# The first tile's z transposed by four DMA transfers from ScalarE's queue, in place of 32 products by the identity

## Chip, core and metric

One core of a Trainium2 chip runs the whole kernel as one program. The metric is the device time in microseconds of one execution; the time before is the median of three.

## What is computed

The input x is 2048 tokens of 512 channels in fp32. Three layers follow each other, each with a residual: `x += 0.5*ffn(layernorm(x))`, then `x += s4(layernorm(x))` (a causal convolution along the channels with a kernel computed from the state-space parameters), then the same ffn again. The ffn is

```python
def _qlinear(x, q, scale, A, Bm):
    w = (q.astype(jnp.float32) - Q_ZERO) * (scale * Q_STEP)[:, None]
    return jnp.einsum('bsh,oh->bso', x, w) + LR_SCALE * (x @ A @ Bm)
g = _qlinear(x, gate_q, gate_scale, gate_A, gate_B)
u = _qlinear(x, up_q, up_scale, up_A, up_B)
h = jax.nn.silu(g) * u
return _qlinear(h, down_q, down_scale, down_A, down_B)
```

with H = 512, I = 1376 and rank 32. The weights q arrive as int32 values of 0 to 15.

## The kernel before

The program is written by hand, one instruction list for each engine, with semaphores between them; nothing is scheduled by a planner, so the order in each list is the order of execution. The 2048 tokens form four tiles of 512, each of four sub-tiles of 128 tokens; the two ffn layers make eight passes, `tile(0)` to `tile(7)`. Every fp32 operand of a product is split into a high and a low fp16 part, so each product runs twice. Tile 0 runs plain products (`plain_blocks`); from tile 1 on a seven-product scheme over 2x2 halves is used (`fast_blocks`), for which the weight sums are made during tile 0.

The normalized input, called z, has tokens on the partitions and has to be turned, so that channels lie on the partitions, before TensorE (PE) can multiply it by the weights. From tile 1 on the turning is done by DMA transposes that SyncE (SP) issues (`quarter_transpose`, L413 to L420). In tile 0 it is done on TensorE: for each sub-tile j VectorE (DVE) makes the fp32 z (`ln_scale`, L915), ScalarE (ACT) rounds it to the high part (`z_first_high`, L848), DVE subtracts to get the low part (`ln_low`, L923, which raises `f.z16`), TensorE multiplies the eight 128x128 blocks by an identity into one bank of PSUM (`x_transpose`, L1407), and one copy brings the 128x1024 result to `xT_plain` in SBUF: ACT's `x_out` (L697) for sub-tiles 0 and 2, DVE's `x_out` (L928) for 1 and 3. `f.xT0[j]` tells that a sub-tile is there.

Around it lies the start of the program. SP loads x, then the int32 weights in four chunks, the low-rank matrices and the constants, all from its own DMA queue (L355 to L386) while the first tile runs. ACT issues four small loads from its own queue at its very start (L646 to L649). TensorE runs `warm`, products of the identity by itself that nobody reads, until z is there (L1732 and L1734). Then it runs, in the order of L1735 to L1749: `p_product(0, i)` (eight products of one turned sub-tile by the low-rank A), `first_products(j)` (the sixteen products of one turned sub-tile with the first block of gate and of up weights) and `p_transpose`. After them `plain_blocks(0)` begins at L1541 with products over all 512 tokens (`product`, L1537).

What ties the engines there: ACT's list from L876 to L892 is `z_first_high`, `low_rank_a_high`, `x_out`, `cast_up` (int32 weights to fp16, L865, which waits for its chunk), `p_high` (three small copies of one low-rank result, L655, waits for `p_product`), `low_rank_b_high`, `p_out` (copies a turned p, L673) and again `cast_up`. `p_transpose(j)` on TensorE waits for `p_out(j-1)` (L1451), and the last of the four low-rank products waits for `p_split(0, 0)` on DVE, which waits for `p_high(0, 0)`. So TensorE cannot enter `plain_blocks(0)` before ACT has done `p_out(1)`, which stands last but one in ACT's list of the start.

## Time and profile before

| | |
|---|---|
| median of 3 runs | 569.65 us (569.47 to 571.22) |
| the profiled execution's own time | 569.99 us |
| its span, first to last instruction | 568.2 us |
| what lies around the span | 1.8 us |
| TensorE busy / VectorE / ScalarE / GpSimd | 556.5 / 427.2 / 312.9 / 256.4 us |

The busy time of TensorE is counted from modelled ends of pipelined products; the chain of waits shows in what order the work that ended last was released. Times are counted from the first instruction. Rows that end in SPq or ACTq are DMA issues: their duration is the time for which the issuing engine's sequencer was held, and the time to landing is counted from the start of the issue.

### The profile page before, as it was taken

What the parts mean: (1) busy time and instruction counts of PE and PEld (TensorE: products, weight loads), DVE (VectorE), ACT (ScalarE), POOL (GpSimd) and SP (SyncE); (2) the same over time, 40 slices, a digit from 0 to 9 for tenths busy, and PEclk for the clock granted to TensorE, in tenths of its full rate; (3) what the DMA queues carried; (4) which work ended last, traced back from release to release, by engine and by line L of the source; (5) the groups of instructions that cost most, each with busy time, mean ns of one, the idle gap of its engine ahead of it and who ended that gap; (6) DMA issues with size and microseconds to landing.
All of it is one profiled execution on the core that took longest, in us unless ns stands there. A gap on an engine that the chain in (4) does not pass through costs nothing.

```text
span 568.2 us, 12661 instructions
## 1 busy us (share of the span) xinstructions
PE 556.5 (98%) x4816; PEld 449.4 (79%) x4816; DVE 427.2 (75%) x824; ACT 312.9 (55%) x773; POOL 256.4 (45%) x272
## 2 busy tenths in 40 slices
PE   8999999989999999999999999999999999999997
PEld 8644678887688877888778887788877888788975
DVE  5789889996889957889578884598845987555544
ACT  5778425863168831688317883178731676246621
POOL 4379612664036850368503784037830477015510
PEclk9999999999999999999999999999999999999999
DMA  8985431009050190002900029000391104440002
GB/s 262 340 282 204 86 59 43 2 1 131 15 22 5 30 180 15 2 2 35 175 16 2 1 38 171 15 3 1 59 151 55 37 2 56 84 158 2 2 0 75
DMA packets 90804, 40.04 MB, mean 70 GB/s; under 512 B 79000, under 2 KB 84889, under 8 KB 90745
## 3 DMA queue, kind: packets, MB, share of 16 engines
q1 hardware_dynamic: 89849, 38.97, 31.3%
q8 instruction: 38, 0.62, 0.5%
q10 hardware_dynamic: 896, 0.27, 0.2%
q14 instruction: 21, 0.17, 0.1%
HBM read 15.90 MB, written 4.19 MB: 35 GB/s over the span
## 4 chain that ended last, share of the span: by engine, by line
PE 92%; DVE 5%; issue 1%; ACT 1%; DVEq 1%; POOL 0%; POOLq 0%; ACTq 0%
PE banks L1561 40%; PE banks L1480 28%; PE banks L1523 6%; PE banks L1537 5%; PE banks L1706 5%; PE banks L1432 2%; PE banks L1716 2%; PE banks L1500 1%; PE banks L1517 1%; PE banks L1726 1%; DVE X L1050 0%; DVE c_stats L1080 0%; DVE ring L1047 0%; DVEq L909 0%; PE banks L1415 0%
## 5 line engine op out<-in xcount | busy, mean ns | idle before, releaser
L1561 PE MATMUL banks<-xT,w 128*128 128x256 f16 (+1 forms) x2156 | 260.4, 273 | 1.5 <-DVE work L1006 1.4
L1561 PEld LDWEIGHTS banks<-xT,w 128*128 128x128 f16 (+1 forms) x2156 | 212.5, 100 | 26.3 <-DVE work L1006 2.7
L1480 PE MATMUL banks<-dw,hT 128*128 128x256 f16 (+3 forms) x1408 | 184.0, 286 | 0.0
L1480 PEld LDWEIGHTS banks<-dw,hT 128*128 128x128 f16 (+1 forms) x1408 | 135.4, 98 | 33.8 <-issue 0.4
L1006 DVE SCALAR_TENSOR_TENSOR work<-banks,work 128x512 f32<-128x512 f32 (+1 forms) x88 | 60.6, 688 | 43.4 <-PE banks L1523 27.4
L501 POOL TENSOR_TENSOR rstd<-veps,minus_half 128x1 f32<-128x1 f32 x32 | 19.6, 615 | 160.8 <-DVE veps L912 160.7
L571 POOL TENSOR_SCALAR hT<-work 128x512 f16<-128x512 f32 x70 | 44.2, 631 | 99.6 <-DVE work L1006 99.6
L574 POOL TENSOR_TENSOR hT<-work,hT 128x512 f16<-128x512 f32 x70 | 82.6, 1179 | 5.8
L1020 DVE SCALAR_TENSOR_TENSOR banks<-banks,scales,work 128x512 f32<-128x512 f32 (+1 forms) x77 | 57.7, 750 | 0.7 <-PE banks L1561 0.7
L1027 DVE SCALAR_TENSOR_TENSOR banks<-banks,scales,work 128x512 f32<-128x512 f32 (+1 forms) x77 | 57.7, 750 | 0.2 <-ACT work L807 0.2
L581 POOL TENSOR_TENSOR z<-zs,z 128x1024 f16<-128x1024 f32 (+1 forms) x28 | 55.5, 1992 | 4.5 <-ACT z L740 4.4
L793 ACT ACTIVATE work<-banks,scales 128x256 f32<-128x256 f32 (+1 forms) x77 | 36.6, 475 | 32.5 <-PE banks L1561 32.5
L807 ACT ACTIVATE work<-banks,scales 128x256 f32<-128x256 f32 (+1 forms) x77 | 36.5, 474 | 31.2 <-PE banks L1561 31.1
L686 ACT ACTIVATE pd_stack<-banks 128x32 f16<-128x32 f32 x96 | 11.8, 195 | 69.2 <-PE banks L1480 69.2
L723 ACT ACTIVATE work<-banks 128x512 f32<-128x512 f32 (+1 forms) x77 | 46.0, 597 | 5.7 <-PE banks L1523 5.7
L789 ACT ACTIVATE work<-banks,scales 128x256 f32<-128x256 f32 (+1 forms) x77 | 36.5, 474 | 7.4 <-PE banks L1561 7.4
L1537 PE MATMUL banks<-xT,w 128*128 128x512 f16 (+1 forms) x160 | 37.9, 379 | 0.6 <-ACT work L716 0.5
L694 ACT ACTIVATE PdT<-banks 128x128 f16<-128x128 f16 x32 | 8.9, 277 | 50.9 <-PE banks L1491 50.8
L796 ACT ACTIVATE work<-banks,scales 128x256 f32<-128x256 f32 (+1 forms) x77 | 36.5, 474 | 0.0
L996 DVE SCALAR_TENSOR_TENSOR pd_stack<-banks,pd_stack 128x32 f16<-128x32 f32 x32 | 6.0, 186 | 35.6 <-ACT pd_stack L686 35.4
L740 ACT ACTIVATE z<-zs 128x512 f16<-128x512 f32 (+1 forms) x56 | 29.8, 568 | 3.0 <-DVE zs L942 2.0
L1537 PEld LDWEIGHTS banks<-xT,w 128*128 128x128 f16 (+1 forms) x160 | 15.5, 100 | 19.8 <-ACT work L716 3.1
(191 smaller groups left out, 677.2 us busy)
## 6 DMA issues: line engine op xcount, KB each, us to landing
out_x<-X SPq DMA_DIRECT2D x15, 256.0 KB, 2.8
X<-in_x SPq DMA_DIRECT2D x1, 2048.0 KB, 9.9
ring<-in_gate_q_t SPq DMA_DIRECT2D x2, 768.0 KB, 9.5
hT<-in_up_q_t SPq DMA_DIRECT2D x2, 768.0 KB, 11.3
X<-in_b SPq DMA_DIRECT2D x2, 560.0 KB, 10.7
X<-in_x SPq DMA_DIRECT2D x1, 1024.0 KB, 14.3
ring<-in_down_q_t SPq DMA_DIRECT2D x1, 1024.0 KB, 12.5
X<-in_x SPq DMA_DIRECT2D x3, 256.0 KB, 5.0
```

Of the source, the lines that this page charges most:

```text
L571: pool.tensor_scalar(hT[0:r, m, 0, :], h32[0:r, b, :], 1.0, 0.0, ALU.mult, ALU.add)\
L574: pool.tensor_tensor(hT[0:r, m, 1, :], h32[0:r, b, :], hT[0:r, m, 0, :], ALU.subtract)\
L581: pool.tensor_tensor(z16[:, j, 1, ops, :], zs[:, ops, :], z16[:, j, 0, ops, :], ALU.subtract)\
L723: nc.scalar.activation(silu[0:r, b, :].rearrange("p (c t) -> p c t", c=2), gate_sums(m), ACT.Silu, scale=LR_OUT).then_inc(f.silu[b], 1)
L789: nc.scalar.activation(t_up[s][0:r, 0, :], sums, ACT.Copy, scale=scales[0:r, 1, m:m + 1])\
L793: nc.scalar.activation(t_gate[s][0:r, 1, :], bank[4 * s + 1][0:r, 0:HH], ACT.Copy, scale=scales[0:r, 0, m:m + 1]).then_inc(f.t5, 1)
L1006: V.scalar_tensor_tensor(shape(h32[0:r, b, :]), up, H_SCALE * LR_OUT, shape(silu[0:r, b, :]), ALU.mult, ALU.mult).then_inc(f.h[b], 1)
L1020: V.scalar_tensor_tensor(up_sums(m), up_sums(m), scales[0:r, 1, m:m + 1], t_up[s][0:r, :, :], ALU.mult, ALU.add).then_inc(f.up_s, 1)
L1027: V.scalar_tensor_tensor(gate_sums(m), gate_sums(m), scales[0:r, 0, m:m + 1], t_gate[s][0:r, :, :], ALU.mult, ALU.add).then_inc(f.gate_s, 1)
L1480: last = mm(acc(j)[:, 1 - c, 0:width], hT[0:rows[m], m, a, j * P:(j + 1) * P], dw[0:rows[m], m, src], start=(m == 0 and a == 0), stop=(m = ...
L1537: last = mm(dst[0:r, :], wg[:, c, cols], xT_plain[:, a, c, :], start=(c == 0 and a == 0), stop=(c == KH - 1 and a == 1))
L1561: last = mm(dst[0:r, 0:HH], w[:, blocks + k, cols], xT[:, a, 2 * op + k, :], start=(first and k == 0 and a == 0), stop=(k == 1 and a == 1) ...
```

## The change

The four `x_transpose` of TensorE, its wait on `f.xT0`, and the four `x_out` copies of ACT and DVE go. ACT issues, for each sub-tile, one DMA transpose of the 128x1024 fp16 sub-tile (`x_turn`), once `f.z16` tells that its two parts are there. Two of them stand behind the second `z_first_high`, two behind the fourth; `cast_up(0)`, the third and the fourth `z_first_high` are put in other places. TensorE's two runs of `warm` become one of 124, and `first_products(0)` moves ahead of `p_product(0, 1)`. The semaphores of a landed sub-tile count to 16. The wait of tile 1's first `z_high` on the last of the transposes becomes four waits on the landed sub-tiles.

```diff
--- before.py
+++ after.py
@@ -294,7 +294,7 @@
 
                 self.z_d, self.z_t = s("z_differences"), s("z_sums")
                 self.zq_hi, self.zq_lo = s("z_quarters_hi"), s("z_quarters_lo")
-                self.tp0, self.xT0 = s("first_x_transposed"), [s(f"first_xT{j}_ready") for j in range(4)]
+                self.xT0 = [s(f"first_xT{j}_ready") for j in range(4)]
                 self.xT = [s(f"xT_sub{j}_ready") for j in range(4)]
                 self.xTq = two("xT_quarters_ready")
                 self.p_b11, self.p_sum = s("p_b11_copied"), s("p_summed")
@@ -694,12 +694,12 @@
                 nc.scalar.activation(PdT[:, j * P:(j + 1) * P], aux[:, 0:P // 2].bitcast(F16), ACT.Copy)\
                     .then_inc(f.pd_out, 1)
 
-            def x_out(j, k, bank_t):
-
-                act.wait_ge(f.tp0, k + 1)
-                nc.scalar.activation(xT_plain[:, :, :, j * P:(j + 1) * P],
-                                     bank[bank_t][:, :].bitcast(F16).rearrange("p (a k t) -> p a k t", a=2, k=KH),
-                                     ACT.Copy).then_inc(f.xT0[j], 1)
+            def x_turn(j):
+
+                act.wait_ge(f.z16, j + 1)
+                act.dma_start(xT_plain[:, :, :, j * P:(j + 1) * P].rearrange("p a k t -> p (a k) t"),
+                              z16_plain[:, j, :, :].rearrange("p a h -> p (a h)"), transpose=True)\
+                    .then_inc(f.xT0[j], 16)
 
             def scaled(accum, g, m):
                 return nc.scalar.activation(accum, accum, ACT.Copy, scale=scales[0:rows[m], g, m:m + 1])
@@ -730,7 +730,8 @@
                 if i == 0:
                     act.wait_ge(f.zs, k)
                     if n == FAST:
-                        act.wait_ge(f.tp0, TS)
+                        for turned_x in f.xT0:
+                            act.wait_ge(turned_x, 16)
                     else:
                         act.wait_ge(f.xTq[j], 32 * (n - FAST))
                 elif i == 1:
@@ -876,15 +877,17 @@
             z_first_high(0)
             low_rank_a_high()
             z_first_high(1)
-            x_out(0, 0, 2)
+            x_turn(0)
+            x_turn(1)
+            z_first_high(2)
             cast_up(0)
-            z_first_high(2)
+            z_first_high(3)
+            x_turn(2)
+            x_turn(3)
             p_high(0, 0)
-            z_first_high(3)
             p_high(0, 1)
             low_rank_b_high(0)
             low_rank_b_high(1)
-            x_out(2, 2, 2)
             p_high(0, 2)
             p_out(0)
             cast_up(1)
@@ -924,13 +927,6 @@
                 dve.wait_ge(f.zhi, n * TS + j + 1)
                 V.tensor_tensor(z16_plain[:, j, 1, :], zs_plain[:, j % 2, :], z16_plain[:, j, 0, :], ALU.subtract)\
                     .then_inc(f.z16, 1)
-
-            def x_out(j, k, bank_t):
-
-                dve.wait_ge(f.tp0, k + 1)
-                V.tensor_copy(xT_plain[:, :, :, j * P:(j + 1) * P],
-                              bank[bank_t][:, :].bitcast(F16).rearrange("p (a k t) -> p a k t", a=2, k=KH))\
-                    .then_inc(f.xT0[j], 1)
 
             def z_apply(n, j):
 
@@ -1380,12 +1376,10 @@
             x_stats(3)
             ln_low(0, 1)
             ln_scale(0, 2)
-            x_out(1, 1, 3)
             ln_scale(0, 3)
             ln_low(0, 2)
             ln_low(0, 3)
             p_split(0, 0)
-            x_out(3, 3, 3)
             p_split(0, 1)
             dve.wait_ge(s_scale_in, 16)
             V.tensor_scalar(scales[:, :, :], scales[:, :, :], Q_STEP / (Z_SCALE * LR_OUT), None, ALU.mult)\
@@ -1404,23 +1398,11 @@
         def _(pe):
             mm = nc.tensor.matmul
 
-            def x_transpose(j, k, bank_t):
-
-                pe.wait_ge(f.z16, k + 1)
-                if k >= 2:
-                    pe.wait_ge(f.xT0[k - 2], 1)
-                dst = bank[bank_t][:, :].bitcast(F16).rearrange("p (a k t) -> p a k t", a=2, k=KH)
-                for a in range(2):
-                    for c in range(KH):
-                        last = nc.tensor.transpose(dst[:, a, c, :], z16_plain[:, j, a, c * P:(c + 1) * P],
-                                                   ident16[:, :])
-                last.then_inc(f.tp0, 1)
-
             def p_product(n, i):
 
                 s = sub(n, i)
                 if n == 0:
-                    pe.wait_ge(f.xT0[i], 1)
+                    pe.wait_ge(f.xT0[i], 16)
                 else:
                     pe.wait_ge(f.xTq[i // 2], (n - FAST + 1) * 32)
                 if n > FAST or (n == FAST and i):
@@ -1717,7 +1699,7 @@
 
             def first_products(j):
 
-                pe.wait_ge(f.xT0[j], 1)
+                pe.wait_ge(f.xT0[j], 16)
                 cols = slice(j * P, (j + 1) * P)
                 for g, wg in enumerate((gw, uw)):
                     pe.wait_ge((s_gcast, s_ucast)[g], 1)
@@ -1729,17 +1711,12 @@
                     if j == TS - 1:
                         last.then_inc((f.g_mm, f.u_mm)[g], 1)
 
-            warm(96)
-            x_transpose(0, 0, 2)
-            warm(28)
-            x_transpose(1, 1, 3)
+            warm(124)
             pe.wait_ge(s_aw, 1)
             p_product(0, 0)
+            first_products(0)
             p_product(0, 1)
-            first_products(0)
-            x_transpose(2, 2, 2)
             first_products(1)
-            x_transpose(3, 3, 3)
             p_product(0, 2)
             p_transpose(0)
             first_products(2)
```

## Rows read from the trace of the kernel before

**Rows 1.** The page: busy time of the engines, chain by engine.

```profile
PE 556.5 (98%) x4816; PEld 449.4 (79%) x4816; DVE 427.2 (75%) x824; ACT 312.9 (55%) x773; POOL 256.4 (45%) x272
...
PE 92%; DVE 5%; issue 1%; ACT 1%; DVEq 1%; POOL 0%; POOLq 0%; ACTq 0%
```

**Rows 2.** TensorE's waits over the whole span: us, times, longest.

```profile
PE banks L1453 <- ACT PT L676: 0.6, 1, 0.6
```

**Rows 3.** The chain in order of time, 10 to 21 us.

```profile
12.06 0.46 PE banks L1415 x8
...
12.55 0.70 DVE xT L931
...
19.22 0.48 ACT p_stack L667 x3
19.70 0.28 ACT PT L676
...
20.12 0.27 PE banks L1453 x2
```

**Rows 4.** Timeline of ACT, 10 to 21.5 us: start, us, what.

```profile
10.67 1.01 ACT L700 ACTIVATE xT<-banks 128x1024 f16<-128x1024 f16 x1
...
15.29 1.02 ACT L700 ACTIVATE xT<-banks 128x1024 f16<-128x1024 f16 x1
...
17.85 1.50 ACT L868 ACTIVATE w<-hT 128x1536 f16<-128x1536 int32 x1
...
19.54 0.44 ACT L676 ACTIVATE PT<-banks 128x256 f16<-128x256 f16 x1
```

**Rows 5.** Busy time of each engine in the stretch 10.13 to 19.98 us.

```profile
10.13:19.98 9.85, 9.03 (x159) 8.69 (x156) 7.85 (x16) 8.66 (x24) 5.22 (x6) 1.00 1.07 365
```

**Rows 6.** DMA transposes of SP, line by line: duration ns min/median/max of the issue.

```profile
L434 SPq DMA_TRANSPOSE ring<-ring x16: 1232/1792/1996, 190.6 to 417.1; - x16
...
DMA to landing us min/median/max: 3.0/3.5/4.0
```

**Rows 7.** The same for the transposes of z of later tiles.

```profile
L418 SPq DMA_TRANSPOSE xT<-z x28: 1373/1581/3287, 61.2 to 484.9; - x28
```

**Rows 8.** Timeline of SP, 128 to 139 us.

```profile
128.61 9.55 SPq L418 DMA_TRANSPOSE xT<-z  x4
```

**Rows 9.** Timeline of SP, 12.8 to 20.3 us.

```profile
12.87 2.00 SPq L365 DMA_DIRECT2D hT<-in_up_q_t  x1
...
16.63 3.66 SPq L378 DMA_DIRECT2D w<-in_omega  x2
```

**Rows 10.** The landing of ACT's load of the low-rank A, 128 KB.

```profile
L648 ACTq DMA_DIRECT2D z<-in_a x1: 451/451/451, 2.0 to 2.0; - x1
...
DMA to landing us min/median/max: 5.5/5.5/5.5
```

**Rows 11.** DMA packets of one transpose of a sub-tile, 190.5 to 194.5 us.

```profile
q1 hardware_dynamic: 1056, 0.26, 35.4%
```

**Rows 12.** Timeline of POOL, 9 to 27 us.

```profile
16.88 1.47 POOL L508 TENSOR_SCALAR w<-ring 128x1536 f16<-128x1536 int32 x1 [3.52 <-DMA hT<-in_up_q_t]
```

**Rows 13.** ACT's own last DMA issue, of the scales.

```profile
L649 ACTq DMA_DIRECT2D scales<-in_scales x1: 528/528/528, 2.4 to 2.4; - x1
```

**Rows 14.** DMA packets by queue, 5 to 7 us (q1 is SP's, q10 ACT's).

```profile
q1 hardware_dynamic: 286, 0.51, 69.7%
q10 hardware_dynamic: 635, 0.14, 32.9%
```

**Rows 15.** Busy time in 2 us windows of the start, PEclk in the seventh column.

```profile
2.00:4.00 2.00, 2.00 (x20) 2.00 (x21) 0.24 (x1) 1.00 (x1) 0.00 (x0) 1.00 0.85 149
4.00:6.00 2.00, 2.00 (x22) 2.00 (x21) 0.79 (x3) 1.14 (x3) 0.56 (x1) 1.00 0.70 220
6.00:8.00 2.00, 2.00 (x27) 2.00 (x26) 1.49 (x5) 0.83 (x2) 0.38 (x1) 1.00 1.07 354
8.00:10.00 2.00, 2.00 (x39) 2.00 (x37) 1.89 (x5) 1.25 (x3) 1.29 (x2) 1.00 1.10 356
```


## Prediction

> **What bounds the kernel now.** I read the page first. TensorE is busy for 556.5 of 568.2 us and 92% of the chain that ended last lies on it [rows 1]: what delays TensorE's work anywhere is paid in full, unless TensorE waits later for something that does not move with it. So I listed TensorE's waits next. Over the whole kernel they are few and short, none of them, after the first products, is for a DMA, and the one in the stretch of this change is the 0.6 us for ACT's copy at L676 [rows 2]. There is nothing later that would absorb a late start. Everything therefore hangs on one time: when the first product of `plain_blocks(0)`, L1537, starts. It is 20.23 us now.
>
> The chain in order of time says what sets that. It runs over TensorE's products by the identity (0.46 us net for the eight of a sub-tile), DVE's copy of 0.70 us, TensorE again, and just before 20.23 us over ACT: `p_high(0, 3)` and `p_out(1)`, L667 and L676, then the two turned products of L1453 at 20.12 us [rows 3]. The timeline of ACT shows what stands ahead of that last copy: two `x_out` copies of 1.01 and 1.02 us, the cast of the second chunk of 1.50 us, and `p_out(1)` ending at 19.54 + 0.44 = 19.98 us [rows 4]. In the 9.85 us from the second `z_first_high` at 10.13 us to there ACT is busy for 8.66, so it has 1.19 us of idle time in all [rows 5]. ACT is nearly full in just the stretch into which four DMA issues are put.
>
> **What goes.** TensorE loses 32 products, 4 x 0.46 = 1.8 us, in a stretch where it also waits. DVE loses two copies of 0.70 us. ACT loses 2.03 us of copies. The two `warm` runs have as many products together as the one run of 124: nothing.
>
> **What comes.** Four issues of DMA transposes in ACT's list. An issue holds the sequencer of the engine that makes it, so what follows on ACT waits behind it: casts, `p_high`, `p_out`. SP issues transposes of exactly this size, 128x1024 fp16, in later tiles: 1.23 us at least, 1.79 at the median, 2.00 at most, landing after 3.0 to 4.0 us [rows 6]. The larger ones of z reach 3.29 us [rows 7], and four of these one after another take 9.55 us, 2.39 each, because each stands behind the packets of the one before [rows 8]. None of these rows ran against a full load of other transfers. Here SP issues the weights meanwhile, and its own issues take 2.00 us and, for two, 3.66 us [rows 9]. I take 2.2 us for one, the middle of 2.00 (the largest of this size) and 2.39 (four in a row), since the four come in close pairs and against a loaded set of DMA engines. The ends are 1.23 and 3.29.
>
> ACT's balance up to the end of `p_out(1)`: +4 x 2.2 = 8.8, less the copies of 2.03, less the idle 1.19, if all of that is filled: 8.8 - 3.2 = **+5.6 us**. With the ends of the issue it is 4.9 - 3.2 = +1.7 and 13.2 - 3.2 = +10.0 us.
>
> **The path over the landings.** The fourth issue ends where `p_high(0, 0)` may start. From there to the end of `p_out(1)` ACT has about 5.0 us of work (four `p_high` of some 0.45 us, two low-rank casts of 0.4, two `p_out` of 0.4, the cast of 1.50), so the fourth issue starts about 7.2 us ahead of that end. The last low-rank product (0.6 us) has to follow the landing and precede the last `p_high` and `p_out` (0.9 us). So landings up to about 5.7 us after their issue are hidden behind ACT. The unloaded rows say 3.0 to 4.0. A load of 128 KB that ACT issued beside SP's took 5.5 us [rows 10], just inside. I cost it at nothing; if that cover is gone, the second rival applies.
>
> **Edits at nothing.** `first_products(0)` before `p_product(0, 1)`: both are TensorE's and both precede the wait for ACT. The new place of the casts and of `z_first_high` costs what ACT's balance already counts. The four waits of tile 1's first `z_high` come some 25 us after the last landing. SP's list keeps all waits and its own transposes come 35 us later. The transposes take some 5 us of all DMA engines' time from SP's loads (4 x 35.4% of the 4 us window [rows 11] is 5.7 us). GpSimd's cast of the second chunk waits 3.52 us for its load and starts at 16.88 us [rows 12], and `cast_up(1)` of ACT follows at 17.85; both users are moved by a like amount, so nothing is added. Without that cover it would be the difference, a microsecond at most.
>
> **The sum.** The profiled execution took 569.99 us, 0.34 above the median of the three. Against it the sum is 575.6; against the median, 569.65 + 5.6 = 575.2 us, and this I forecast. Its own range by the ends is 571.3 to 579.7.
>
> **A rule against the change.** Turned on TensorE, a sub-tile costs 0.46 us net and one copy of 0.7 to 1.0 us [rows 3, 4], and a transfer lands after 3.0 us at best [rows 6]. The Trainium skill says the same for a single block (page "VectorE: DVE Perf Modes", sections "The three transpose paths" and "Rules for kernel authors"): transpose 128x128 on TensorE if a PSUM destination is acceptable, by the DMA crossbar otherwise. Its figures for one 128x128 block are 1309 ns by DMA and 390 ns on TensorE; an estimate from these figures of the Trainium skill alone, with nothing overlapped, would be 32 x 0.92 = 29 us slower. The rows disagree on the size, with 3.0 to 4.0 us for eight blocks at once, and the sum goes by them.
>
> **Rivals.**
>
> *Not slower: ACT's queue issues them cheaply.* ACT's own plain issues hold it for 0.53 us [rows 13]. If a transpose from ACT costs no more, the balance is 2.1 - 3.2 = -1.1 us, and TensorE, with 1.8 us less to do, could use it: 568.5 us. It decides below (2.03 + 1.19) / 4 = 0.8 us an issue. Against it stands that no transpose of any size was issued in under 1.2 us here [rows 6, 7]. Chance 5%.
>
> *Landings bind.* ACT's packets share the DMA engines with the loads. From 5 to 7 us, with both queues full, ACT's got 635 packets through, 318 in a microsecond, and SP's 286 [rows 14]. A sub-tile's transpose has 1056 [rows 11], so four need 4224/318 = 13.3 us; from a first packet at about 11.6 us they end at 24.9, and L1537 follows 1.7 us later (low-rank product, `p_high`, `p_out`, turning): 26.6, +6.4 us, hardly other than the forecast. If instead each packet of the transposes alternates with one of the load, 77 ns and 18 ns by the shares of [rows 14], that is 168 in a microsecond, 25 us, and +18. Midway, 243, gives 17.4 us and +10.5: 580.1 us. Chance 15%.
>
> *The descriptor generator is shared.* SP's issues of 2.00 and 1.8 us stand back to back from 12.87 to 20.3 us [rows 9]. If only one queue can issue at a time, three of ACT's four wait for one of SP's, about 2.2 us each: 6.7 more, +12.3 us, 581.9. No row shows ACT and SP issuing against each other in this stretch. The Trainium skill has it so ("Perfetto Trace Analysis", section "DMA Instruction — HWDGE (DVE, Sync)"): the generator is locked for exclusive use from one issue's start to the end of its descriptors, and the wait for the lock counts as part of the issue. Chance 12%.
>
> *TensorE's clock falls.* After `warm` TensorE is idle from about 11.6 us until the first landing, and then works in pieces. At the start it ran 20, 22 and 27 products in 2 us windows, and 39 from then on [rows 15]: 48 fewer at 51 ns, 2.5 us, is the price of once going from the lower level to 2.4 GHz. Were it paid again in `plain_blocks(0)`, the time would be 569.65 + 5.6 + 2.5 = 577.7 us. For it: TensorE would have no product for over 2 us before the first landing. Against: the granted clock reads 1.00 in all these windows, though also in those with few products, so it tells little of the start. Chance 17%.
>
> **How the numbers follow.** The forecast has 43%, the rivals 5, 15, 12 and 17; the remaining 8% is the cheap end, 1.7 us or less, with nothing else. What a measurement of this kernel can tell from no change is 0.3%, 1.7 us. Faster needs issues well under 0.8 us: 4%. Within 0.3%, from that and the cheap end: 7%. Slower: 89%. The range runs from just under the cheap end, 571.0, to the shared generator, 582.0; the two outer rests and the first rival are what is left out.
>
> **What would show it.** Right: four ACTq issues of `x_turn` of about 2.2 us each, `p_out(1)` ending near 25.6 us, the first L1537 near 25.9, TensorE's order and busy time from there on as before, each landing under 5.7 us. Wrong: landings of 8 us and TensorE waiting for a DMA (landings bind); issues of 4 us (shared generator); L1537 products at twice their time after 25 us (clock); issues of 0.5 us (the other side). It would also be wrong if a wait later in tile 0 closed the gap, which [rows 2] excludes.

## The result and the profile after

The changed kernel takes **594.1 us** (median of four, 593.0 to 598.1) against 570.0 us (median of four of the kernel before, 569.5 to 571.2): a ratio of 1.0429, 95% interval 1.0406 to 1.0451, so slower by 4.3%. The forecast was 575.2 us, and the range ended at 582.0. The profiled execution of the changed kernel took 593.02 us and spans 591.2, 23.0 more than before. Of the kernels in the experiments, one had, beside four executions near 578 us, a fifth of 969.9 us at a mean granted clock of 0.56, which is in none of the medians here.

The page of the changed kernel: its span, busy time, and the chain that ended last by engine.

```profile
span 591.2 us, 12597 instructions
...
PE 561.4 (95%) x4784; PEld 452.7 (77%) x4784; DVE 424.7 (72%) x822; ACT 311.2 (53%) x771; POOL 258.2 (44%) x272
...
PE 84%; DVE 5%; DMA 2%; issue 2%; ACT 2%; DVEq 0%; ACTq 0%
```

TensorE has 32 products fewer, as the diff says, yet 4.9 us more of busy time than in [rows 1], since many of them run at half the clock, as shown below; "DMA 2%" is new in the chain. The waits of TensorE name the transfer (us in all, times, longest):

```profile
PE banks L1414 <- DMA xT<-z: 17.6, 4, 10.7
...
PE banks L1519 <- ACT work L716: 1.1, 2, 0.6
PE banks L1519 <- DVE work L1002: 0.7, 1, 0.7
```

[Rows 2] have no DMA in their place. L1414 is `p_product`, which wants a turned sub-tile; it waits at all four. The second and third line, in `plain_blocks(0)`, are new or longer too; they come back below. The timeline of ACT (start, us, what, and the idle time before it) shows the issues:

```profile
10.03 8.41 ACTq L700 DMA_TRANSPOSE xT<-z  x2
18.49 0.63 ACT L851 ACTIVATE z<-zs 128x512 f16<-128x512 f32 x1 [7.83 <-issue]
...
19.88 4.04 ACTq L700 DMA_TRANSPOSE xT<-z  x1
...
23.95 4.52 ACTq L700 DMA_TRANSPOSE xT<-z  x1
28.52 0.81 ACT L667 ACTIVATE p_stack<-banks 128x64 f16<-128x64 f32 x6 [7.94 <-issue]
...
39.60 0.40 ACT L676 ACTIVATE PT<-banks 128x256 f16<-128x256 f16 x1
```

`p_out(1)` ended at 19.98 us in [rows 4] and ends at 40.00 here. The answer for line L700 alone gives the durations of the issue (ns, min/median/max) and the time from issue to landing:

```profile
L700 ACTq DMA_TRANSPOSE xT<-z x4: 1364/4280/6770, 10.0 to 24.0; - x4
...
DMA to landing us min/median/max: 12.5/13.6/16.0
```

The same transfer landed after 3.0 to 4.0 us in [rows 6]. In the chain in order of time, the way from the last landing to the block runs over TensorE alone, with no issue and no copy of ACT in it:

```profile
20.58 3.37 issue
23.95 13.93 DMA xT<-z
...
37.93 1.03 PE banks L1414 x8
...
41.10 2.04 PE banks L1519 x7
```

And this is what the two queues did from 22 to 24 us and from 16 to 18 us (packets, MB, share of 16 engines; q1 is SP's with the weights, q10 ACT's with the transposes):

```profile
q1 hardware_dynamic: 416, 0.62, 85.0%
q10 hardware_dynamic: 416, 0.11, 24.0%
...
q1 hardware_dynamic: 182, 0.70, 89.9%
q10 hardware_dynamic: 181, 0.05, 10.8%
```

**One packet of the load for one of the transposes**, nearly to the packet. A packet of the load carries about 1.5 KB from 22 to 24 us (0.62 MB / 416) and 3.8 KB from 16 to 18 us, one of a transpose 256 bytes; the two counts stay equal whatever the size. So the transposes get through at the pace of the load's packets: 91 in a microsecond beside the largest, 208 beside those of 1.5 KB (and 227 from 34 to 36 us), some 180 on the whole (4224 packets between 14 and 37.4 us), where [rows 11] had the 1056 of a sub-tile through in a 4 us window with nothing beside.

**Where the 23.0 us of span come from.** The first product of `plain_blocks(0)` starts at 40.89 us, 20.66 later than the 20.23 of before. Three steps of the prediction's own path over the landing make up the difference. In that path the fourth issue starts 7.2 us ahead of the end of `p_out(1)`, at 18.4 us, the landing is covered for 5.7 us, and the block starts at 25.9:
- the first three issues take 1.36 + 6.77 + 4.04 = 12.2 us where 3 x 2.2 were forecast, so the fourth starts at 23.95 in place of 18.4: +5.55;
- it lands 13.93 us after its issue in place of within 5.7: +8.23;
- from that landing to the block 3.01 us go by in place of 1.8: +1.21, since TensorE's clock is at its lower level there.

25.9 + 5.55 + 8.23 + 1.21 = 40.89. The windows of 10 us from 10 to 40 us (busy time of PE, PEld, DVE, ACT, POOL, then PEclk) show the third:

```profile
10.00:20.00 10.00, 1.88 (x34) 1.70 (x31) 3.98 (x7) 2.14 (x4) 4.80 (x6) 0.74 1.10 325
20.00:30.00 10.00, 5.00 (x46) 4.76 (x47) 1.28 (x4) 1.99 (x10) 3.77 (x3) 0.50 1.13 329
30.00:40.00 10.00, 5.49 (x51) 4.96 (x49) 1.21 (x4) 2.83 (x9) 5.38 (x10) 0.50 1.09 330
```

The granted clock is 0.50, its lower level of 1.2 GHz, after a stretch of 10.7 us in which TensorE had nothing to do, and 0.51 over the whole of 14 to 42 us. The rest, from +20.66 to +23.0, is lost later in tile 0. The timeline of TensorE shows it in two products of the block:

```profile
70.55 1.90 PE L1519 MATMUL banks<-xT,w 128*128 128x512 f16 x8
...
80.55 1.93 PE L1519 MATMUL banks<-xT,w 128*96 128x512 f16 x8 [0.65 <-ACT work L716]
```

Their counterparts before, in its timeline:

```profile
49.49 1.90 PE L1537 MATMUL banks<-xT,w 128*128 128x512 f16 x8
...
57.27 1.89 PE L1537 MATMUL banks<-xT,w 128*96 128x512 f16 x8
```

That is +21.06 and +23.28: 2.2 us more in ten microseconds, long after the last transpose and at full clock.

### The profile page after: what moved, and what is told of

It reads as the page before. It is cut to its first block, busy times and chain, and to the rows that moved or that the text cites. A ratio compares the mean times of both kernels' runs of the same rounds, so it can differ in the third digit from the quotient of the medians.

```text
span 591.2 us, 12597 instructions
## 1 busy us (share of the span) xinstructions
PE 561.4 (95%) x4784; PEld 452.7 (77%) x4784; DVE 424.7 (72%) x822; ACT 311.2 (53%) x771; POOL 258.2 (44%) x272
## 4 chain that ended last, share of the span: by engine, by line
PE 84%; DVE 5%; DMA 2%; issue 2%; ACT 2%; DVEq 0%; ACTq 0%
PE banks L1543 38%; PE banks L1462 27%; PE banks L1505 6%; PE banks L1688 4%; PE banks L1519 3%; DMA xT<-z 2%; PE banks L1414 2%; PE banks L1482 1%; DVE hT L1008 1%; DVE work L1002 1%; ACT banks L705 0%; PE banks L1499 0%; ACT work L716 0%; DVE X L1046 0%; DVE c_stats L1076 0%
## 5 line engine op out<-in xcount | busy, mean ns | idle before, releaser
L686 ACT ACTIVATE pd_stack<-banks 128x32 f16<-128x32 f32 x96 | 11.8, 195 | 70.3 <-PE banks L1462 70.3
L1414 PE MATMUL banks<-a_w,xT 128*128 128x128 f16 x256 | 21.2, 230 | 18.3 <-DMA xT<-z 17.6
L1414 PEld LDWEIGHTS banks<-a_w,xT 128*128 128x128 f16 x256 | 17.7, 103 | 20.9 <-issue 11.8
## 6 DMA issues: line engine op xcount, KB each, us to landing
hT<-in_up_q_t SPq DMA_DIRECT2D x2, 768.0 KB, 12.5
```

The costliest lines, as they stand in the source:

```text
L1414: last = mm(p_bank(n, i)[:, out * 4 * R:(out + 1) * 4 * R], x, a_w[:, c, :], start=(t == 0), stop=(t == len(terms) - 1))
```

## The experiments

Theory A says that the two queues take turns on the DMA engines packet for packet, and that the long issues are the same thing seen from ACT: the queue takes no more because its packets do not leave. Its rivals are that ACT's issues are slow of themselves or wait for a shared descriptor generator, so that ACT's list sets the start; and that the clock costs most of it.

### Without the load beside the transposes

SP holds the second chunk of weights and all behind it until the fourth sub-tile has landed.

```diff
             for c in range(2):
+                if c == 1:
+                    sp.wait_ge(f.xT0[3], 16)
                 chunk(c)
```

> The changed kernel, but SP issues the second chunk of weights and all later loads only when the fourth sub-tile has landed. Theory A (the packets of the two queues take turns one for one on the loaded DMA engines, so the landings are slow because of the loads): the four issues take at most 2.0 us each, each lands within 4.5 us, the first product of plain_blocks(0) starts near 25 us instead of 41; the held chunk then lands near 31 us and is cast near 33, so about +7 to +9 us against the kernel before, 577 to 579. Theory B (ACT's queue is slow in itself, whatever runs beside it): issues of 4 to 7 us stay, and the time is 594 or more. Theory C (the half clock of TensorE is most of the loss): the idle time before the first landing stays over 2 us, so the clock falls all the same and the time stays over 588.

Measured: 582.28 us (581.5 to 583.1), ratio to before 1.0211 (1.0153 to 1.0270), about 12 us under the changed kernel. The line of the issues, the landings, and TensorE's two waits:

```profile
L702 ACTq DMA_TRANSPOSE xT<-z x4: 1247/1298/1926, 10.1 to 16.6; - x4
...
DMA to landing us min/median/max: 3.2/3.5/4.3
```

```profile
PE banks L1437 <- ACT PT L678: 5.6, 1, 5.6
PE banks L1416 <- DMA xT<-z: 3.3, 1, 3.3
```

The same four instructions of the same engine now hold ACT for 1.25 to 1.93 us and land after 3.2 to 4.3, the prices of [rows 6]. ACT's queue had 1201 packets through in two microseconds, by the DMA view of 16 to 18 us, alone on the engines:

```profile
q10 hardware_dynamic: 1201, 0.30, 81.7%
```

600 in a microsecond alone, 208 beside the load: both the hold and the landing come from what SP does beside them, as theory A has it. The run takes away SP's issues together with its packets, so by itself it does not tell the load from a shared generator; the rows for that stand under "The descriptor generator is shared" below. What is left of the slowdown is the price of the experiment: `cast_up(1)` waits for the held chunk until 26.4 us, `p_out(1)` stands behind it in ACT's list, and TensorE waits 5.6 us for that and enters the block at 28.80 us, 8.6 late. After this idle time the granted clock is 0.50 from 28 to 36 us, the first two runs of eight products take 3.62 and 3.59 us in place of 1.89 and 1.90, and at the third, at 38.22 us, the kernel is 12.7 us late. The expectation had neither the length of the wait nor the clock in it, hence a time above it.

### The transposes beside an unchanged path

To the kernel before, four transposes from ACT are added at the places that the change gives them, into memory that nobody reads. TensorE's own transposes and all copies stay.

```diff
             x_out(0, 0, 2)
-            cast_up(0)
+            turn_spare(0)
+            turn_spare(1)
             z_first_high(2)
-            p_high(0, 0)
+            cast_up(0)
             z_first_high(3)
+            turn_spare(2)
+            turn_spare(3)
+            p_high(0, 0)
```

> The kernel before, whose z is still turned by TensorE, with four DMA transposes from ACT at the places of the change that write to unused memory and for which nobody waits until 40 us. It prices the hold on ACT alone. Theory A: the issues take together 15 to 17 us as in the changed kernel, p_out(1) ends near 34 us, so +13 to +15 us against before, 583 to 585; the remaining 6 to 7 us of the 20.7 at the first block are the wait for the fourth landing. If the hold were harmless and the landings were all: within 3 us of before.

Measured: 588.29 us (588.0 to 588.6), ratio 1.0317 (1.0266 to 1.0368). The issues, and TensorE's waits:

```profile
L888 ACTq DMA_TRANSPOSE X<-z x2: 1556/4124/6691, 10.7 to 12.3; - x2
L888 ACTq DMA_TRANSPOSE work<-z x2: 3645/3928/4211, 21.1 to 24.8; - x2
```

```profile
PE banks L1451 <- ACT xT L707: 6.4, 1, 6.4
PE banks L1745 <- ACT w L877: 6.1, 1, 6.1
```

Nobody waits for a landing before 40 us, and still the block starts at 36.37 us, 16.1 later than before. The two effects stand side by side and are not a sum: with the hold of ACT alone (16.1 us of issues) the block is 16.1 us late, TensorE's lower clock included (0.64 from 20 to 36 us); in the changed kernel the landings come a few microseconds behind it and set the end. I had expected some 14 us in all and got 18. Of these, 2 us come after the start of the block, by the same waits as in the late start below.

### The same transposes from SP's queue

`x_turn` moves from ACT's list to SP's, ahead of the second chunk.

```diff
             for c in range(2):
+                if c == 1:
+                    for j in range(TS):
+                        x_turn(j)
                 chunk(c)
```

> The changed kernel with the four transposes issued by SP, ahead of the second chunk of weights, in place of ACT. ACT is not held and no load is in flight beyond the first chunk. Theory A: landings 3 to 4.5 us after each issue, the last near 19 to 20 us, plain_blocks(0) starts within 2 us of the kernel before, and the second chunk, issued near 17 us instead of 6, lands near 27: +3 to +5 us against before, 573 to 575. Theory B (only ACT's queue is slow): the same. A time over 580 would be against both.

Measured: 579.48 us (578.4 to 580.6), ratio 1.0162 (1.0095 to 1.0230), above what was expected. SP's four issues take 1232/1289/1336 ns (min/median/max) and land after 3.1 to 3.9 us: as from ACT with the load held. So neither queue is slow of itself. Again TensorE waits 5.3 us for `p_out(1)` behind `cast_up(1)`, and its first eight products of the block then take 3.62 us. Two further versions took that wait away. The first has, on top of this edit:

```diff
             p_high(0, 3)
             p_out(1)
+            cast_up(1)
```

> The kernel whose transposes SP issues ahead of the second chunk, with ACT's cast of that chunk moved behind the last p_out of the start. In the earlier run TensorE waited 5.3 us for a p_out that stood behind this cast. Theory: that wait goes, plain_blocks(0) starts near 21 us, the third block waits for the cast until 26 or 27 us: +1 to +3 us against before, 571 to 573. If the held loads bound it anyway: 577 or more.

Measured: 577.84 us (577.6 to 581.5, median of four), ratio 1.0136 (1.0116 to 1.0156); the profiled execution is the one of 581.47. The block now starts at 21.30 us, only 1.07 later than before, since ACT issues nothing, and then TensorE waits 3.4 us for `p_out(2)` and 1.7 us for the state-space parameters, both from held loads, and its clock falls (0.57 from 28 to 36 us). The second moves these parameters ahead of the transposes and the cast behind `p_out(3)`:

```diff
                 if c == 1:
+                    for half in range(2):
+                        at = slice(half * NS, (half + 1) * NS)
+                        sp.dma_start(state[at, :], state_d[:, 0:9]).then_inc(s_kin, 16)
...
                         p_out(3)
+                        cast_up(1)
```

> The kernel whose transposes SP issues ahead of the second chunk, with the four small loads of the state ahead of them as well, and ACT's cast of the second chunk behind the fourth p_out, in tile 0's first block. In the run before TensorE waited 3.4 us for the third p_out behind the cast and 1.7 us for the state. Both waits should go: plain_blocks(0) at 21.3 us as there, +1 to +3 us against before, 571 to 573. It can't be faster than before: its first block starts 1.1 us later.

Measured: 578.16 us (576.9 to 579.3), ratio 1.0123 (1.0102 to 1.0144), no better. The wait moved once more: `cast_up(1)` itself waits for its chunk until 25.7 us, and the block's own work waits 2.3 us for ACT; TensorE's clock falls again (0.50 from 32 to 36 us), and one run of eight products takes 3.49 us. Both expectations, 571 to 573, failed for the same two reasons: loads held for the transposes are late for the block, wherever the cast stands, and the waits for them bring the lower clock. No arrangement that I tried pays for the transposes.

### Smaller packets of the load

If the turns are packet for packet, and not by bytes, the transposes must gain when the load's packets shrink, though the load's bytes stay. The weights are loaded block by block, in rows of 128 int32, 512 bytes.

```diff
-                sp.dma_start(gq_raw[:, :, cols], gq_v[:, :, cols]).then_inc(s_q[c], 16)
-                sp.dma_start(up_raw[c], uq_v[:, :, cols]).then_inc(s_q[c], 16)
+                for m in range(m0, m1):
+                    to = min((m + 1) * P, I)
+                    sp.dma_start(gq_raw[:, :, m * P:to], gq_v[:, :, m * P:to]).then_inc(s_q[c], 16)
...
```

> The changed kernel, its weights loaded in pieces of one block of 128 columns: the same bytes in packets of 512 B in place of 1408 and 1536 B. Theory A (one packet of the transposes for one of the loads, whatever its size): the pairs get shorter, so from 20 us on ACT's queue passes clearly more than the 208 to 227 packets a microsecond it had, near 300, the fourth landing comes at 30 to 34 us in place of 37.9, and the kernel takes 586 to 591. If the engines shared time or bytes instead of packets, ACT's packet rate and the landings would stay as they were, 594.

Measured: 586.09 us (584.8 to 587.4), ratio 1.0282 (1.0252 to 1.0311), 8 us under the changed kernel though SP has more issues to make; the last sub-tile landed at 32.0 us in place of 37.9. The queues from 28 to 30 us and from 22 to 24 us:

```profile
q1 hardware_dynamic: 746, 0.37, 70.7%
q10 hardware_dynamic: 801, 0.20, 50.8%
...
q1 hardware_dynamic: 782, 0.49, 117.7%
q10 hardware_dynamic: 58, 0.01, 6.5%
```

From 26 to 28 us (624 to 619) and from 28 to 30 us ACT's queue passes 312 and 400 packets in a microsecond in place of 208 and 227, near one to one: there it is the number of packets that is shared, and not bytes or time. The expectation was met, but this kernel has stretches that the rule does not cover. From 18 to 20 us ACT's queue passed 926 packets to SP's 222, and from 20 to 24 us 144 to 1041. Up to 24 us ACT's queue had sent 2134 packets, those of two transposes (2112) and hardly one of the third, which was issued at 17.45 us. So packets that come late, some 6 us after their issue, are here a large part of the 8.9 to 12.6 us to a landing, beside the turns. Why they come late is open.

### One transpose alone

The kernel before, with the fourth sub-tile alone turned by ACT's DMA.

```diff
             z_first_high(3)
+            x_turn(3)
             p_high(0, 1)
```

> The kernel before with only the fourth sub-tile turned by a DMA transpose from ACT; the others stay on TensorE. Theory A: one transpose of 1024 packets at about 200 a microsecond, behind the load of the low-rank B: landing 7 to 10 us after its issue at about 14.5 us, the issue itself 1.2 to 2 us since nothing stands behind it; the first product of plain_blocks(0) near 25 us, +4 to +6 us, 574 to 576. If the loss were a matter of having several transposes queued on each other: under +2 us.

Measured: 581.86 us (581.3 to 582.4), ratio 1.0208 (1.0187 to 1.0228): a quarter of the change costs half of the slowdown. The issue held ACT for 1.41 us, since nothing of its own queue stood before it, and landed after 10.3 us. From 20 to 22 us:

```profile
q1 hardware_dynamic: 412, 0.57, 85.1%
q10 hardware_dynamic: 410, 0.10, 25.1%
```

That is the one-to-one rule again, with a short issue and a long landing: it is the second and later issues that are held, behind packets of their own queue. The block starts 8.2 us late: TensorE waits 3.9 us for the landing and 2.5 us for ACT's `x_out` of the third sub-tile, which stands behind the issue, and works at half the clock in between (1.92 us for the sixteen products that took 1.06). The expectation was too low by some 6 us. I had priced the packets but not that the first of them would go out late, past 19 us, after an issue at 15.1. Of the 11.8 us, 3.6 come after the start of the block; which wait is which there is left open.

### The clock

TensorE is given products that nobody reads for its gaps, 310 ahead of the first landing and 60, 64 and 50 between the others. They write to another bank of PSUM than the 124 of the changed kernel did.

```diff
-            warm(124)
+            warm(310)
             pe.wait_ge(s_aw, 1)
...
             first_products(0)
+            warm(60)
             p_product(0, 1)
             first_products(1)
+            warm(64)
...
             first_products(2)
+            warm(50)
```

> The changed kernel with more products of the identity by itself: 310 in place of 124 at the start, and 60, 64 and 50 in TensorE's waits for the second, third and fourth landing. Only TensorE's clock differs. Theory A: the landings stay where they are, near 22.5, 27.7, 33.1 and 37.9 us, the clock stays at 1.00 and the products between the last landing and plain_blocks(0) take half as long: 1.5 to 2.5 us less than the changed kernel, about 592. Theory C: 10 us less or more, under 584.

Measured: 596.52 us (596.3 to 596.7), ratio 1.0461 (1.0411 to 1.0511): no gain over the change, whose own runs reach from 593.0 to 598.1. The clock part did nearly as expected: PEclk is 1.00 from 10 to 20 and from 30 to 50 us and 0.83 between, where TensorE still waits 4.0 us for the first landing, and from the last landing to the block 1.9 us go by in place of 3.0. But the last sub-tile landed at 43.3 us, 5.4 later (one profile of each kernel). The DMA view from 18 to 20 and from 20 to 22 us shows how:

```profile
q1 hardware_dynamic: 379, 0.52, 81.5%
q10 hardware_dynamic: 382, 0.10, 31.0%
...
q1 hardware_dynamic: 130, 0.09, 98.4%
q10 hardware_dynamic: 129, 0.03, 35.6%
q8 instruction: 1, 0.02, 3.4%
```

Both queues fall to 65 packets in a microsecond, together, next to one packet of the instruction queue, and again at 30 to 32 us (135 and 133), and from 40 to 41 us (21 and 21), each time during or just behind such a fetch. That more instructions need more fetches was the guess behind the next run: the same cover with a quarter of the added products, each of 512 columns. The first 124 stay narrow; 47, 15, 16 and 12 wide ones follow.

```diff
+                four = ident16[:, :].unsqueeze(1).broadcast_to([P, 4, P])
                 for _ in range(count):
-                    mm(bank[7][:, P:2 * P], ident16[:, :], ident16[:, :], start=True, stop=True)
+                    mm(bank[2][:, :], ident16[:, :], four, start=True, stop=True)
```

> The products without readers of the earlier run that kept TensorE's clock up, made with 512 columns each: as much of TensorE's time in a quarter of the added instructions. In that run both queues' packets fell to about 65 a microsecond three times, each time beside an instruction fetch of 16 KB. If these fetches cost it its landings (43.3 instead of 37.9 us): fewer dips, the fourth landing back near 38 us, and 590 to 593, some 2 us less than the changed kernel. If it is TensorE's activity itself that slows the transfers: landings near 43 and 596 as before.

Measured: 594.04 us (593.6 to 594.4), ratio 1.0421 (1.0400 to 1.0442), the same as the changed kernel and above the 590 to 593 that I expected. One dip behind a fetch is left (130 and 122 packets from 34 to 36 us, the fetch from 33 to 34), one more of a microsecond has no fetch beside it (67 and 66 from 20 to 21 us), and the last landing is at 40.2 us. The landing moved the right way and not far enough. In the changed kernel the clock is worth 1.2 us at the start of the block and 0.6 us in its first eight products (2.47 against 1.89 us); what its fall costs elsewhere, the runs with held loads show.

### A late start alone

The 2.2 us that are lost between 70 and 81 us come some 30 us after the last of the four transposes. In the kernel before, 370 products that nobody reads stand ahead of `plain_blocks(0)`, so that it starts as late as in the changed kernel, at full clock and without any transpose.

```diff
             p_transpose(2)
+            for _ in range(370):
+                mm(bank[2][:, P:2 * P], ident16[:, :], ident16[:, :], start=True, stop=True)
             for n in range(N2):
```

> The kernel before with 370 products without readers, 20.6 us, just ahead of plain_blocks(0): TensorE starts it as late as in the changed kernel, while loads and transposes are those of before. It tells the 20.7 us at the first block from the 2.4 us that the changed kernel loses later in tile 0. If a late start alone moves DVE's and GpSimd's work onto each other there: +22 to +24 us, 592 to 594, with DVE's subtraction for h at 2 us and more beside GpSimd's for z. If those 2.4 us come from the loads that the transposes delayed: +20.6, 590.7.

Measured: 593.60 us (593.1 to 594.1), ratio 1.0401 (1.0375 to 1.0427). The block starts 21.3 us late, and the counterpart of the product of 57.27 us is 23.4 us late, as in the changed kernel (23.3). The timelines of VectorE and GpSimd of this kernel:

```profile
70.19 2.61 DVE L1012 TENSOR_TENSOR hT<-work,hT 128x512 f16<-128x512 f32 x1
```

```profile
69.62 2.63 POOL L581 TENSOR_TENSOR z<-zs,z 128x1024 f16<-128x1024 f32 x1
```

The same happens once more at 75 us (2.13 us). In the kernel before, the same subtraction of VectorE takes 1.09 us in VectorE's timeline:

```profile
49.04 1.09 DVE L1012 TENSOR_TENSOR hT<-work,hT 128x512 f16<-128x512 f32 x1
```

There GpSimd's subtraction starts only at 53.06 us and falls beside other work of VectorE. In the late kernel, as in the changed one (70.10, 2.61 us, with GpSimd from 69.54), the two fall on each other: GpSimd's subtraction has moved by 16.6 us and TensorE's products by 21. The PSUM bank comes free late, and TensorE waits. The 2.2 us are a consequence of the late start, of whatever cause: the same loss comes without any transpose at the start.

### The kernel before with the cast moved

The move of `cast_up(1)` that took the wait ahead of the block out of SP's version might also help the kernel before.

```diff
             p_out(0)
-            cast_up(1)
             p_high(0, 3)
             p_out(1)
+            cast_up(1)
```

> The kernel before with ACT's cast of the second chunk, 1.50 us, moved behind the last p_out of the start; nothing else. TensorE's wait of 0.6 us for that p_out should go and plain_blocks(0) start 0.6 to 0.9 us earlier; the cast then ends near 21 us, still 4 us before its block. 0.5 to 0.9 us faster than before, 569.1 to 569.5; if the scaling behind the cast becomes the wait, no difference.

Measured: 570.36 us (median of 12, 569.4 to 572.9), against 570.33 (17 runs) of the kernel before on the same chip; ratio 1.0008 (0.9994 to 1.0022), no difference. TensorE's timeline:

```profile
19.18 1.89 PE L1537 MATMUL banks<-xT,w 128*128 128x512 f16 x8
21.87 0.27 PE L1453 MATMUL banks<-ident,p_stack 128*128 128x128 f16 x2 [0.80 <-ACT PT L676]
```

The block starts 1.05 us earlier and gives it back three microseconds later, waiting for `p_out(2)` behind the moved cast. No version beat the kernel before.

## Why the prediction was wrong

**The bound.** Right: the time hangs on the start of `plain_blocks(0)`, and nothing later absorbs a late start, though something later adds to it. Of the 23.0 us of span, 20.7 are there at the first product.

**"What goes".** Right, and without weight: 1.8 us of TensorE's work, in a stretch where it now waits 17.6 us.

**The step that failed: the price of an issue, and above all "the path over the landings".** The issue was put at 2.2 us, with 3.29 as its outer end, and a landing at 3.0 to 4.0, "hidden" up to 5.7. All those rows were of transposes that ran where no full load ran beside them. The prediction says that of them itself and then takes the values all the same; the wait for a landing stood in the sum at nothing. Measured beside the load: 1.36, 6.77, 4.04 and 4.52 us, 16.7 in all against 8.8, and 12.5 to 16.0 us to the landing. With the load held, the prices of those rows come back (1.25 to 1.93, and 3.2 to 4.3 us). The rows were right for their place and had been carried to another. How the two divide: the fourth issue ended at 28.47 us in place of 18.4 + 2.2 = 20.6, so by ACT's list alone the block would have started near 33.8, an estimate from these rows, 13.5 us late; the wait for the fourth landing and the clock behind it make the other 7.1.

The one bound that was taken from a loaded stretch, 5.5 us for a load of 128 KB at the start [rows 10], did not reach far enough either: it ran in a stretch where ACT's queue had 635 packets to SP's 286 [rows 14]. The one row with both queues in it had them two to one, though the engines' time was full in it too (69.7% and 32.9%). So one to one is what the windows of the changed kernel from 16 to 36 us show and not a rule for every stretch; that a queue without packets waiting on every engine makes the difference is a guess.

**"Landings bind".** The right mechanism, at 15%, and mis-sized. Its outer end was this case: one packet for one, 168 in a microsecond, 25 us, +18. It was priced midway between that and the 318 of [rows 14], at +10.5, and the range stopped below the outer end. The midpoint of two laws is a law that nobody proposed: either ACT's packets go at their own pace or they take turns, and the runs have them take turns (416 to 416). With 168 in a microsecond the last landing would be at 36.6 us; it was at 37.9. (The shares of [rows 14] give 78 and 17 ns for the two packets where the prediction has 77 and 18, and the same 168.) That the estimate comes so close is in part luck: the first packets go out some 4 us after the issue in place of 1.6, and from then on some 180 pass in a microsecond; the two errors nearly cancel, and the 180 is a mean over windows of a microsecond that from 16 us on pass 90 to 252, with the size of the load's packets.

The Trainium skill had the rule by which to choose. Its page "DMA: Bandwidth & Descriptors", section "Queues, rings and completion order", says that each DMA engine takes turns between the queues it has work for, packet by packet. The trace agrees from 16 to 36 us: 416 to 416. On the Trainium skill's page "Advanced Engine Details and Errata", section "X-Bar Transpose (TRN2)", transposes are as fast as regular transfers. The trace does not agree in bytes: in the best microsecond with nothing beside them, the load held, they moved 0.21 MB (835 packets, the engines' time full), and the load alone moves 0.37 MB in one (12 to 13 us of the kernel before); beside packets of 1.5 KB they moved 0.05.

**"The descriptor generator is shared."** It named issues of 4 us as its mark, and issues of 4 us came, for another reason. While ACT's second issue was open, from 11.67 to 18.44 us, SP made four of its own, and while the fourth was, from 23.95 to 28.47 us, it made these three and most of a next one, in SP's timeline:

```profile
24.06 0.64 SPq L383 DMA_DIRECT2D work<-in_down_b  x1
24.73 0.62 SPq L383 DMA_DIRECT2D d_scale<-in_down_scale  x1
25.40 1.31 SPq L364 DMA_DIRECT2D ring<-in_gate_q_t  x1
```

So an open issue of ACT did not keep SP from issuing. Nor is it SP's issues that make ACT's long: the single transpose, issued beside two of SP's in a row, of 2.17 and 2.19 us, took 1.41 us; the long ones are those behind an earlier transpose of the same queue. The mark in the list of what would show it was not one that told the two apart.

**"TensorE's clock falls."** It fell, for longer than the prediction has it, and cost 1.8 us in place of 2.5. A rival in the list became a small term of the sum, beside the others and not in their place.

**"Not slower."** Fell: no issue of a transpose was under 1.2 us in any run.

**"Edits at nothing".** GpSimd and the casts: right, GpSimd's casts of the second and third chunk start 0.9 and 1.8 us later (17.76 and 27.13 us in place of 16.88 and 25.37) and bind nothing. The loss of 2.2 us near 70 us is missing from the prediction altogether. "TensorE's order and busy time from there on as before" does not hold when TensorE moves by 21 us and GpSimd by 16.5.

## What to carry to other kernels

Take the price of a transfer from a row with the same company: a transfer of many small packets beside a load of large ones goes at the large ones' pace in these traces, and the engine that issues several such transfers is held for the difference. Ask of every duration in a sum what ran beside it, and where two laws give its ends, price each of them as a case. A crossbar transpose belongs where the DMA engines are empty, as in the later tiles of this kernel; at the start, under the weights' load, products by the identity are far cheaper.

## What the runs showed of the hardware beyond that

- In the changed kernel from 16 to 36 us the two queues share the DMA engines packet for packet, not byte for byte: 416 to 416 with packets of 256 bytes and some 1.5 KB, 181 to 182 beside 3.8 KB. With the load in smaller packets it is 624 to 619 in one window and 58 to 782 in another, so it is not so in every stretch. SP's queue loses a sixth by it: 0.62 MB in two microseconds beside the transposes against 0.74 MB without, before.
- An issue is long when packets of the same queue are waiting and hardly leave: 1.36 us for the first, 6.77 for the second beside the load, but four in a row from SP's queue at 1.23 to 1.34 with the later loads held.
- The first packets of a transpose go out late beside a load: some 4 us after the issue in the changed kernel and in the one with a single transpose, some 6 us for the third in the kernel with small packets. Why is open; the packets already queued ahead of it on SP's side are a guess that no run tested.
- With transposes in flight, a fetch of instructions goes with about 2 us in which both queues fall to some 65 packets in a microsecond: three times with the narrow products added, once with the wide ones, once with the spare transposes (145 and 147 from 36 to 38 us). Beside a fetch with only loads, 12 to 13 us and 22 to 23 us before, SP's queue passes 244 and 227. This rests on times that coincide, there is a dip without a fetch as well (wide products, 20 to 21 us), and the mechanism was not tested.
- VectorE's fp32 subtraction of 128x512 takes 2.61 us beside GpSimd's subtraction of 128x1024, against 1.09 us where GpSimd makes casts meanwhile and 0.68 us at 32.44 us in the kernel before, beside GpSimd's multiplication of 128x256 by a column.
